# A graph layer and a mixture of experts on one core: three list blocks by one-hots, and the start of the edge loop in another order

## What is computed

```python
x = x + relu(segment_sum(edge_weight[:, None] * (layernorm(x) @ W)[src], dst, 1024) + bias)
t = layernorm(x)                                   # nx
scores = sigmoid(x @ Wg.T + bg)                    # the input of this part is layernorm(x)
w, idx = top_k(scores, 2);  w = w / w.sum(-1)
h = silu(nx @ W1p[e] + b1p[e]) * (nx @ W3p[e] + b3p[e])    # W1p = gamma[e] * W1[e], b1p = b1 + beta[e] @ W1[e]
y = sum over the two experts of w * (h @ W2[e] + b2[e])
z = (silu(nxs @ Ws1 + bs1) * (nxs @ Ws3 + bs3)) @ Ws2 + bs2    # nxs = nx * gs + bs
out = x + y + z
```

## Time and profile before

| | us |
|---|---|
| median of 3 runs | 455.81 |
| the runs | 454.72 to 456.16 |
| the profiled execution | 455.27 |
| its span, first to last instruction | 453.5 |

### The profile page before, as it was taken

One profiled execution on the slowest core, in us unless ns is written; L12 is line 12 of the kernel. 1 busy time (PEld: TensorE's weight loads), 2 busy tenths in 40 slices (PEclk: granted clock), 3 DMA queues, 4 the chain that ended last, 5 costly groups with the idle time before them and its releaser, 6 DMA issues.

```text
span 453.5 us, 6577 instructions
## 1 busy us (share of the span) xinstructions
PE 386.7 (85%) x1845; PEld 206.6 (46%) x1846; DVE 206.2 (45%) x680; ACT 166.1 (37%) x412; POOL 155.6 (34%) x262
## 2 busy tenths in 40 slices
PE   1699999999999976899999999988788779688800
PEld 1576776755665544534443444343333333334400
DVE  5879888315666674543223322331231231221136
ACT  9859999313323220223332333232312312313200
POOL 3575453013655561723223322331221221210100
PEclk9999999999999995899999999999999999999965
DMA  4999800010003661299999999999999999997168
GB/s 114 335 356 408 353 0 0 22 35 34 24 26 107 240 234 72 73 364 411 405 408 405 409 405 407 406 407 408 408 408 406 407 404 407 405 404 303 52 229 330
DMA packets 41331, 125.05 MB, mean 276 GB/s; under 512 B 7890, under 2 KB 8466, under 8 KB 41043
## 3 DMA queue, kind: packets, MB, share of 16 engines
q1 hardware_dynamic: 35506, 116.25, 66.4%
q0 software_dynamic: 5792, 8.43, 5.2%
HBM read 119.64 MB, written 13.91 MB: 294 GB/s over the span
## 4 chain that ended last, share of the span: by engine, by line
PE 74%; DVE 8%; issue 7%; DMA 6%; POOL 2%; DVEq 1%; SPq 0%; ACT 0%; ACTq 0%; POOLq 0%
PE bank L1311 26%; PE bank L1341 12%; PE bank L1183 11%; PE bank L1333 5%; PE bank L1151 5%; PE bank L1144 4%; PE bank L1304 3%; DMA slots<-small,GW 2%; PE bank L1171 2%; DMA w<-totals 1%; PE bank L1202 1%; DVE stats L744 1%; DMA A<-slots 1%; PE bank L1251 1%; DVE X L1092 1%
## 5 line engine op out<-in xcount | busy, mean ns | idle before, releaser
L1030 DVE SCALAR_TENSOR_TENSOR osl<-bank,b13T,osl 128x64 f32<-128x64 f32 x128 | 27.5, 277 | 157.8 <-ACT osl L675 157.8
L1311 PE MATMUL bank<-w,xhT 128*64 128x512 f32 x352 | 82.1, 608 | 14.6 <-issue 14.6
L668 ACT COPY xh<-bank 128x512 f32<-128x512 f32 x33 | 19.4, 586 | 147.3 <-PE bank L1311 144.0
L1183 PE MATMUL bank<-HW,AT 128*128 128x512 f32 x128 | 58.2, 592 | 0.0
L1311 PEld LDWEIGHTS bank<-w,xhT 128*64 128x64 f32 x352 | 25.9, 138 | 56.1 <-issue 54.6
L543 POOL DMA_INDIRECT totals<-osl,A x17 | 17.0, 1001 | 84.7 <-PE bank L1304 69.1
L543 POOL DMA_INDIRECT totals<-GW,A x16 | 16.1, 1003 | 83.4 <-PE bank L1304 69.2
L1341 PE MATMUL bank<-w,osl 128*64 128x512 f32 x176 | 41.9, 593 | 0.0
L587 ACT ACTIVATE osl<-iota,eT 128x128 f32<-128x128 f32 x128 | 39.0, 389 | 5.2 <-PE bank L1144 5.2
L539 POOL DMA_INDIRECT A<-nx_rows,A x33 | 34.5, 1047 | 18.0 <-issue 9.6
L1183 PEld LDWEIGHTS bank<-HW,AT 128*128 128x128 f32 x128 | 22.9, 191 | 21.0 <-issue 21.0
(11 more groups left out here) (217 smaller groups left out, 565.2 us busy)
## 6 DMA issues: line engine op xcount, KB each, us to landing
w<-in_L_ffn_W_dram SPq DMA_DIRECT2D x66, 1024.0 KB, 19.6
A<-in_L_ffn_W_dram SPq DMA_DIRECT2D x15, 1024.0 KB, 19.8
HW<-in_L_ffn_W_dram SPq DMA_DIRECT2D x10, 1024.0 KB, 18.3
AT<-in_L_ffn_W_dram SPq DMA_DIRECT2D x5, 1024.0 KB, 20.6
...
```

The source lines that it names most:

```text
L1030: ins = v.scalar_tensor_tensor(hT[b][:, m, CAP * h:CAP * h + CAP], bank[4][:, (HC + m) * P + CAP * h:(HC + m) * P + CAP * h + CAP], b13T[: ...
L1183: ins = t.matmul(bank[4 + s % 2][:, :], AT[:, s % 2, k, :], HW[:, k, :], start=(k == 0), stop=(k == NB - 1))
L1311: ins = t.matmul(bank[2 + b][CAP * h:CAP * h + CAP, :], xe[b][:, c, CAP * h:CAP * h + CAP], up_w[v][:, h, :, c, :], start=(c == 0), stop=( ...
```

## The change

- The list takes blocks 5, 6 and 7 from one-hots (`DRAM_BLOCKS` = 5). The read of the list is issued ahead of the sixth slot. All parts are accumulated in one PSUM range, cleared once, and copied once (`listed`).
- SP issues x blocks 0 and 1, W and the other x blocks first, then the gate rows and small weights. The gate rows lie in the last W2 slot, whose load waits until they are turned, after the edge loop. The bias sum goes into block 1 of the message stage (`shared_bias`).
- PE makes the product of a block ahead of its quads, and turns the next block right after; DVE instead of ACT copies the turned rows. DVE has the statistics in four pieces. POOL makes two of four tiles in three of four quads (one in the first four quads). Clearing `A` is divided among DVE, POOL and ACT.
- PE gets 14, 6 and 4 transposes of a constant in the start (`keep_busy`), and 20 instead of 24 ahead of the first turned rows.
- The first `up` starts after half of its rows (`xe_first`); the rows of pair 1 are turned after it.

```diff
-POOL_M = 1
+A_DVE, A_POOL = 2400, 5300
+def pool_tiles(q, first):
+    return 2 if q % QUAD and not (first and q < QUAD) else 1
...
-        Ws = HW[:, NB - 1, 0:4 * 64].rearrange("p (c n) -> p c n", c=DC)
-        Wsb = AT[:, 1, 4:6, :].rearrange("p a n -> p (a n)").rearrange("p (c n) -> p c n", c=DC)
-        sentinel = HW[:, 0:5, :].rearrange("p b d -> p (b d)")[:, 0:(EXPERTS * LIST + P) * REC // P]
+        Ws = R[:, :, 64:128]
+        Wsb = eT[:, 0:2, :].rearrange("p a n -> p (a n)").rearrange("p (c n) -> p c n", c=DC)
+        sentinel = w13[:, RING - 2:RING, :, :, :].rearrange("p e k c h -> p (e k c h)")[:, 0:(EXPERTS * LIST + P) * REC // P]
...
             xv = x.rearrange("(b p) d -> p b d", p=P)
-            sp.dma_start(X[:, 0:2, :], xv[:, 0:2, :]).then_inc(x_in[0], 16)
+            for i in range(2):
+                sp.dma_start(X[:, i, :], xv[:, i, :]).then_inc(x_in[i], 16)
+            sp.dma_start(GW[:, :, :], W.rearrange("(p c) n -> p c n", c=DC)).then_inc(gw_in, 16)
+            for i in range(1, 4):
+                sp.dma_start(X[:, 2 * i:2 * i + 2, :], xv[:, 2 * i:2 * i + 2, :]).then_inc(x_in[i + 1], 16)
...
-            for i in range(1, 4):
-                sp.dma_start(X[:, 2 * i:2 * i + 2, :], xv[:, 2 * i:2 * i + 2, :]).then_inc(x_in[i], 16)
-            sp.dma_start(GW[:, :, :], W.rearrange("(p c) n -> p c n", c=DC)).then_inc(gw_in, 16)
...
             for v in range(RING // 2):
+                if v == RING // 2 - 1:
+                    sp.wait_ge(sentinel_out, 16)
                 load_up(v, v)
-                load_down(v, v)
+                if v < RING // 2 - 1:
+                    load_down(v, v)
...
+            sp.wait_ge(raw_transposed, 2)
+            load_down(RING // 2 - 1, RING // 2 - 1)
...
                 if s == NB - 2:
+                    for i in range(2):
+                        sp.wait_ge(rec_out[i], 32 * ((DRAM_BLOCKS + 1 - i) // 2))
+                    sp.dma_start(L, lists[:, :, 0:CAP * REC]).then_inc(list_in, 16)
                     sp.wait_ge(out_ps, NB)
                     load_up(RING // 2 + 1, RING // 2 + 1)
                     load_down(RING // 2 + 1, RING // 2 + 1)
-                    for i in range(2):
-                        sp.wait_ge(rec_out[i], 32 * DRAM_BLOCKS // 2)
-                    sp.dma_start(L, lists[:, :, 0:CAP * REC]).then_inc(list_in, 16)
...
+            g.memset(A[:, A_DVE:A_POOL], 0.0).then_inc(a_chain, 1)
...
-            inverse_deviations(range(0, 2), 1)
+            inverse_deviations(range(0, 1), 1)
+            g.memset(sentinel, NOWHERE).then_inc(consts, 1)
+            inverse_deviations(range(1, 2), 2)
...
+                        for k in range(pool_tiles(q, first)):
...
+            pool.wait_ge(a_chain, R1 * QUADS + 4)
...
+            for c in range(DC):
+                ins = g.tensor_scalar(Wsb[:, c, :], Ws[:, c, :], gs4[:, 1, c:c + 1], None, ALU.mult)
+            ins.then_inc(wsb_ready, 1)
+            pool.wait_ge(wsb_ready, 1)
+            for c in range(DC):
+                ins = g.tensor_scalar(Ws[:, c, :], Ws[:, c, :], gs4[:, 0, c:c + 1], None, ALU.mult)
+            ins.then_inc(wsb_ready, 1)
...
-            def x_transposed(g, u):
-                act.wait_ge(xhT_ps, g + 1)
-                a.copy(xhT[:, u, :, :].rearrange("p c n -> p (c n)"), bank[4 + u][:, :]).then_inc(xhT_ready, 1)
...
-            def pair(j, last):
+            def pair(j, first, last):
 
                 half = j * 4
-                x_transposed(j * 2, 0)
-                one_hots(half, j, 2, False)
-                one_hots(half, j, 3, False)
-                x_times_w(j * 2, 0)
-                x_transposed(j * 2 + 1, 1)
+                for u in range(2):
+                    if u:
+                        one_hots(half, j, 2, False)
+                    one_hots(half, j, 2 * u + 1, first)
+                    x_times_w(j * 2 + u, u)
                 if not last:
                     one_hots(half + 4, j + 1, 0, False)
-                    one_hots(half + 4, j + 1, 1, False)
-                    x_times_w(j * 2 + 1, 1)
...
             act.wait_ge(slo_ready, 1)
+            for k in range(8):
+                ins = a.activation(osl[:, 0, k, :], iota[:, :], ACT.Abs, bias=eT[:, 1, k:k + 1])
+                if k == 3:
+                    act.wait_ge(xhT_ps, 1)
+                    a.copy(xhT[:, 0, :, :].rearrange("p c n -> p (c n)"), bank[4][:, :]).then_inc(xhT_ready, 1)
+            ins.then_inc(osl_chain, 1)
+            act.wait_ge(osl_chain, 1)
+            a.activation(osl[:, 0, :, :], osl[:, 0, :, :], ACT.Relu, scale=-1.0, bias=1.0).then_inc(osl_ready, 1)
             act.wait_ge(edges_ready, 1)
...
+                if s == 0:
+                    act.wait_ge(raw_transposed, 1)
+                    a.copy(R[:, :, 0:64], bank[6][:, 0:256].rearrange("p (c e) -> p c e", c=DC)).then_inc(raw_evac, 1)
...
+            v.memset(A[:, 0:A_DVE], 0.0).then_inc(a_chain, 2)
...
+            for b in range(2, 4):
+                c_clear = mark(v.memset(bank[b][:, 0:QW], 0.0))
+            mean_and_variance(range(0, 1))
...
+            def standard_rows(b, u):
+
+                v.tensor_scalar(xh[:, u, :], X[:, ds(b, 1), :].rearrange("p a n -> p (a n)"),
+                                mv[:, ds(b, 1), 0], rstd[:, ds(b, 1)], ALU.subtract, ALU.mult).then_inc(xh_ready, 1)
+
+            dve.wait_ge(rstd_ready, 1)
+            standard_rows(0, 0)
             need(c_row)
...
+            mean_and_variance(range(1, 2))
...
-                dve.wait_ge(quad_done[q % 2], done + (q // 2 + 1))
...
                     v.memset(bank[(q - 1) % 4][:, 0:QW], 0.0).then_inc(zeroed, 1)
+                dve.wait_ge(quad_done[q % 2], done + (q // 2 + 1))
                 v.tensor_tensor(to, to, bank[q % 4][:, 0:QW], ALU.add).then_inc(a_chain, 1)
...
+                    u = q // 4
+                    b = j * 2 + u
+                    for k in range(pool_tiles(q, with_x and first), QUAD):
...
-                    if with_x and first and q == 1:
-                        mean_and_variance(range(2, NB))
+                    if with_x and first and q == 0:
+                        need(c_clear)
+                        v.memset(bank[0][:, 0:QW], 0.0).then_inc(zeroed, 1)
+                        v.memset(bank[1][:, 0:QW], 0.0).then_inc(zeroed, 3)
+                        dve.wait_ge(rstd_ready, 2)
+                        standard_rows(1, 1)
...
+                    if with_x and q % 4 == 3 and not (last and u):
+                        transposed_rows(b + 1, 1 - u)
+                    if with_x and first and q in (3, 4, 6):
+                        c = {3: 2, 4: 4, 6: 6}[q]
+                        mean_and_variance(range(c, c + 2))
+                    if with_x and first and q in (5, 6):
+                        dve.wait_ge(rstd_ready, 3)
+                        standard_rows(q - 3, q - 5)
+                    if with_x and not first and not last and q % 4 == 1:
+                        dve.wait_ge(rstd_ready, 5)
+                        dve.wait_ge(xhT_ps, b + 1)
+                        standard_rows(b + 2, u)
...
-            dve.wait_ge(sums_done, 1)
-            link(v.tensor_tensor(bc[:, 64:128], bc[:, 64:128], bank[7][:, 0:64], ALU.add))
+            link(v.memset(list_bank[:, 0:64], 0.0))
...
-            def listed_first():
-
-                dve.wait_ge(list_ps, 1)
-                link(v.tensor_copy(listed, list_bank[:, 64:128]))
-                v.tensor_tensor(listed, listed, list_bank[:, 0:64], ALU.add).then_inc(listed_ready, 1)
-
-            def listed_last():
-
-                dve.wait_ge(list_ps, 2)
-                dve.wait_ge(listed_ready, 1)
+            def listed():
+
+                dve.wait_ge(list_ps, NB - DRAM_BLOCKS)
                 dve.wait_ge(at_ps, 2 * NB)
-                v.tensor_tensor(TOKDST, listed, list_bank[:, 0:64], ALU.add).then_inc(list_ready, 1)
+                v.tensor_copy(TOKDST, list_bank[:, 0:64]).then_inc(list_ready, 1)
...
+                if s == 1:
+                    dve.wait_ge(sums_done, 1)
+                    dve.wait_ge(small_in, 48)
+                    v.tensor_tensor(bc[:, 64:128], bc[:, 64:128], bank[7][:, 0:64], ALU.add).then_inc(bc_ready, 1)
+                    dve.wait_ge(bc_ready, 1)
...
-            rows(0, 0)
+            dve.wait_ge(xe_ps, 1)
+            tokens = bank[0][:, :].rearrange("p (c h t) -> p c h t", c=DC, h=2)
+            to = xe[0].rearrange("p c (h t) -> p c h t", h=2)
+            for c in (slice(0, 2), slice(2, 4)):
+                link(v.tensor_tensor(to[:, c], tokens[:, c], gT[:, c, 0:2].unsqueeze(3).broadcast_to([P, 2, 2, CAP]), ALU.mult))
+                ins = v.tensor_tensor(to[:, c], to[:, c], bT[:, c, 0:2].unsqueeze(3).broadcast_to([P, 2, 2, CAP]), ALU.add)
+                ins.then_inc(xe_first if c.start == 0 else xe_ready, 1)
...
+            keep_busy(bank[7], 14)
...
+            keep_busy(bank[7], 6)
+
+            def x_rows(g, u):
+
```

(55 more changed lines are left out.)

184 lines of the change are left out of this document (76 added, 108 removed).

## The result

The changed kernel takes **452.05 us** (median of 5 runs, 450.56 to 452.8) against 455.72 us before (5 runs); the ratio is 0.9907, 95% interval [0.9882, 0.9931]. It is faster, by 3.7 us and not by 10.3. The forecast was 445.2 us, with a range to 450.0 us that does not hold the time. The profiled execution took 451.02 us, with a span of 449.1 us against 453.5 us: -4.4 us, and all that follows explains these 4.4 us.

What follows compares the result with a forecast made beforehand. The prediction took the weight stream, restarted by the first `up`, to set the end. Terms -5.5, +0.8, -5.7, -0.8 and +0.9 us summed to -10.3 us from 455.27 us; forecast 445.2 us, range 441.5 to 450.0 us.

Steps and rivals of the forecast that it cites:

- first transpose of A: End of the edge loop: the first A transpose starts at 80.3 us instead of 85.78 us, -5.5 us.
- list, to the gather: List stage: no wait for the list read, block 7's chain last, gather at 174.3 instead of 180.05 us, -5.7 us.
- after the first `up`: Weight stream: pair 1's later turn costs +0.5 us and two scatters moved into the full stretch +0.4 us.
- Rival 1: First `up`: TensorE's clock is at the lower level, so 3.65 us become 7.3 us; 448.8 us, chance 0.15.
- VectorE begins its tiles at 13.5 us: Loop start: keys made at 12.25 us, tiles 1.23 us later, 0.4 us later than before.
- the rule: Edge loop: VectorE in 2-port mode and GpSimd block each other on the shared port; +8 us, 453 us, chance 0.05.
- What counts is then VectorE's work of the first two blocks: First pair of the loop: VectorE's work sums to 18.6 us, so the product of block 2 starts at 32.1 us.
- rival 4: Loop start: TensorE is at 1.2 GHz until the second block, some 3 us; 448 us, chance 0.08.
- I take 7.83 us a block: Edge loop: six blocks left after 32.1 us take 47.0 us, end 79.1 us, with GpSimd's and VectorE's work hidden.
- The 16 gate transposes: After the loop: 1.2 us at the higher clock level, against 1.73 us for 12 at the lower level before.
- A microsecond by which the first `up` comes earlier is a microsecond at the end: Weight stream: its volume is fixed and it restarts when the first `up` ends, so gains there carry to the end.
- rival 6: Weight stream: a hole of its own that only now shows takes up the shift; no change, 455 us, chance 0.02.

Runs made afterwards that it cites:

- e2: Changed kernel with the last three blocks' record scatters behind gathers 12 to 14 and the overflow list loaded at slot 13; 448.55 us.
- e4: Changed kernel with the sentinel filled by ScalarE instead of GpSimd; 449.63 us.
- f3: Changed kernel with sentinel filled by ScalarE, GpSimd tiles one, two, two, one per four quads, and late records behind gathers 12 to 14; 446.3 us.
- f4: Changed kernel with two last blocks going to the list by one-hots, not three; 453.86 us.
- experiment 8: Changed kernel with the sentinel filled by ScalarE instead of GpSimd, the same run as e4; 449.63 us.
- experiments 6 and 7: 6: changed kernel, ScalarE's second one-hot step on half the columns, 776 us, output wrong; 7: f3 with GpSimd making one of eight one-hots, 444.63 us.
- g1: Changed kernel with ScalarE's second one-hot step on half of the columns, output wrong; 15.20 us a pair of blocks, 776 us as a whole.

## Why the prediction was wrong, point by point

By its own steps, in the two profiled executions:

| step | forecast, us | measured, us |
|---|---|---|
| first transpose of A | -5.5 | -1.3 |
| message stage (to the route of block 7, 166.99) | +0.8 | +0.9 |
| list, to the gather | -5.7 | -5.8 |
| gather to first `up` | -0.8 | -1.4 |
| after the first `up` | +0.9 | +3.2 |
| sum | -10.3 | -4.4 |

- **The list and the message stage** were right in size and in mechanism: no wait for the list read, the rows landed in time, block 7's own chain last. Rival 1, a slow clock in the first `up`, did not come in this trace: the 20 transposes took 4.04 us and the first `up` 3.65 us. In e2, e4, f3 and f4 it came in part: 5.2 to 6.3 us, 1.6 to 2.7 us more. That it stayed away in the profiled execution of the changed kernel was luck.
- **"VectorE begins its tiles at 13.5 us"** failed by 1.5 us, at the step "the normalisation of block 0 (about 0.55 us)". I had not looked at what GpSimd does beside it: the sentinel's fill, which the diff moves to just this place. The Trainium skill (SBUF — State Buffer, Who interferes with whom) has the rule; I gave it 0.05, since the earlier trace rows did not bear it out. For the tiles it is still not borne out (three in 0.88 us beside GpSimd's). For the fill and the normalisation the trace agrees: the second ends 0.28 us behind the first, after 2.01 us, and experiment 8 gives 0.53 us without the fill. I asked the rule only in the place for which I had a row.
- **"What counts is then VectorE's work of the first two blocks"** (18.6 us) was short by 1.0 us: from 15.03 to 34.61 us there are 19.6 us, in which VectorE waits 1.93 us, until 21.44 us, for TensorE's first quad. A sum over one engine left out that it needs another at its start. And "I take it that it is fast by the time of the first product" failed: 5.40 us at a granted clock of 0.52, then 1.00, which is a part of rival 4. How much of the 1.0 us this is stays open. The step at 13.5 us and this one are 2.5 us at the third product.
- **"I take 7.83 us a block"** (measured 8.0, +0.8 us in six blocks) named TensorE as the bound and ScalarE as relieved. In the changed kernel ScalarE and its two buffers hold the pace (experiments 6 and 7); taking one copy a block off it left it waiting for its buffers instead. That it was the bound in the kernel before too is argued and not tested: there it is busy for 15.62 of 16.00 us from 36.5 to 52.5 us, which the 41.95 of 48.30 us of the earlier trace rows hide, since they take in the loop's end. "TensorE is busy for 47.35 of 48.30 us" was no proof: its matmuls stretch when they are waited for (in the kernel before, 16 tiles read 1.95 us at 37.95 us and 2.34 us at 56.38 us, at the same granted clock), and its own work for a pair is 15.2 us (g1), not 15.6.
- **The 16 gate transposes** took 2.1 instead of 1.2 us. I had halved their earlier 1.73 us for the clock, though the granted clock read 1.00 there (11.5 to 14 us). Twelve of them take 1.65 us now, 0.14 us each for 64 columns, where a tile of 128 columns takes 0.12 us: they have little to gain from the clock.
- **"A microsecond by which the first `up` comes earlier is a microsecond at the end"**, with +0.4 us for two more scatters, was the costly step: 3.2 us instead of 0.9. The stream's volume is fixed, its length is not. By starting earlier it ran into four scatters, where before three of four lay ahead of the restart. I had given the scatters bounds of 0 and 0.8 us, from no row; the runs show some 3 us for four or five of them (218.1 to 218.8 us from restart to last issue, against 214.5 to 215.9 with none to two). My rival 6 had this mechanism, a hole in the stream that only now shows, at a chance of 0.02 and only for the whole shift.

So 4.2 us were lost ahead of the first transpose of A and 2.3 us behind the first `up`; 0.6 us came back in between. The range was too narrow, because no case in it let two of these go wrong together.
